# Reordering TensorE's queue in the attention stage: the scores of two steps next to each other, ahead of the values

## The chip, the core and the metric

The kernel runs on one core of one Trainium2 chip. The metric is the device time of the whole kernel in microseconds (us), from the first to the last instruction and what lies around them; the kernel has one launch. The engines are TensorE (PE), VectorE (DVE), ScalarE (ACT), GpSimd (POOL) and SyncE (SP), which runs the DMA queue that loads and stores.

## The reference, cut to what matters

Two layers follow each other. The first is a differential attention over 4 batches of 512 tokens with 8 heads, times a gate that comes from a second attention and a mixture of 8 experts. The second layer (a state-space scan and a second mixture) is not touched by the change. The part that the change concerns:

```python
# layer 0, attention, for every batch and head: 512 queries, 512 keys, head size 8 (twice)
L1 = einsum('bhnd,bhmd->bhnm', l2norm(q1), l2norm(k1)) * cos_scale
L2 = einsum('bhnd,bhmd->bhnm', l2norm(q2), l2norm(k2)) * cos_scale
G  = tanh(delta_gain * (L1 - L2))
A1 = softmax(L1 + G);  A2 = softmax(L2 - G)
y  = einsum('bhnm,bhmd->bhnd', A1 - lambda_full * A2, v)
...
# layer 0, mixture of experts, tokens of each expert
h = relu(xf @ W1[e] + b1[e]);  out = out + m * (h @ W2[e] + b2[e])
```

## The kernel before, in words

The second of the kernel's stages computes the attention and, in the same instruction stream, the experts' blocks. Every engine has a written-out order of its own, and semaphores join them. An engine takes its instructions in the order written, so one that waits holds up all behind it.

The work is cut into **steps**, **units** and **passes**. A step is 128 keys by 512 queries of one head and one batch. A unit is four steps, that is all 512 keys of one head and batch; in the code `st` counts steps and `u = st // 4` counts units. A pass is a pair of heads: 8 units, 32 steps. There are four passes, q = -1, 0, 1, 2. The first (q = -1, `first=True`) has no expert blocks beside it, but at its start VectorE also works out where each token's row goes (`route`). Passes 0 and 1 are one hardware loop, pass 2 is written out again with `final=True`. In passes 0 to 2 each unit carries one block of 128 tokens through an expert.

What is done for a step, and by whom:

- TensorE: `difference(st)` computes L1 - L2 into `bank_d[st % 2]` (line 873, one matmul of 112 rows); `scores(st)` computes L1 and L2 into the two halves of `bank_l[st % 2]` (lines 878 and 879, two matmuls of 48 rows that lie in two different halves of the array and run at the same time).
- ScalarE: `gate(st)` is the tanh, `bank_d` to `gt` (line 998).
- VectorE: `sums(st)` computes L1 + G and L2 - G (the second half is stored with its sign turned), from `bank_l` and `gt` into `tt` (lines 1055 and 1056, two instructions).
- ScalarE: `exps_of_two(st)` takes the exponential of two steps in one instruction (line 1005), `tt` to `ex`.

Since there are two banks of scores, `scores(st)` may start only when the sums of step st - 2 are done:

```python
def scores(q, st):                      # on TensorE
    pe.wait_ge(s_T, step(q, st - 1))    # s_T counts sums: those of steps 0 .. st-2 are done
```

For a unit: `weigh(u, pair)` multiplies two steps' exponentials with the values into `bank_pv` (line 927; four matmuls of 32 columns side by side, written as eight instructions; the values of a unit take pair 0 and pair 1). ScalarE's `keep(u)` copies `bank_pv` to `pvs` after pair 1 (line 1010), TensorE's `turn(u)` transposes it back into `bank_pv` (line 935), and VectorE's `settle(u)` reduces it (line 1063). The next unit's `weigh(., 0)` may start only when `settle` is done. In the iteration with number u of the TensorE loop the scores are those of steps 4u+4 to 4u+7, while `weigh` and `turn` belong to unit u-1.

For an expert block: `turn_block` (line 902), ScalarE's `keep_in` (1014), `hidden` (908), VectorE's `relu` (1071), `block_out` (914), ScalarE's `keep_out` (1019), then again `turn_block` of the next block, which uses the same bank and so waits for `keep_out`.

ScalarE's order around the change, for one unit: gates of steps 4u+4 and 4u+5, `keep(u-1)`, exponentials of 4u+2 and 4u+3, `keep_out(u)`, gates of 4u+6 and 4u+7, `keep_in(u+1)`, exponentials of 4u+4 and 4u+5. VectorE's: sums of 4u+4, sums of 4u+5, `settle(u-1)`, sums of 4u+6, sums of 4u+7, `relu(u+1)`. At steps 14 and 30 of a pass a `mean_square` (line 1129) stands between the sums of 4u+6 and of 4u+7, and at steps 5 and 21 a reciprocal (line 1125) behind `settle`.

SyncE loads the operands of the second head of a pass (`second_head`, line 716) behind two of the block loads; POOL prepares a head's values (`next_head`, line 780) when the last unit that reads the old ones has been weighed, and then the rows of the blocks, for which the block loads wait.

Of the kernel before, what the change touches and what calls it, by code (L numbers as in the profile page):

```python
# [46 lines left out]
def build_stages(nc, A, out):  # L47
    keep = ExitStack()
    with keep:
# [25 lines left out]
        with keep0:  # L75
# [561 lines left out]
            with st2:  # L637
# [60 lines left out]
                with nc.Block() as block:  # L698
# [159 lines left out]
                    def _(pe):  # L858
# [3 lines left out]
                        def operands(q, st):  # L862
                            u, mb = st // 4, st % 4
                            i, b = (u // 4) % 2, u % 4
                            if st % 16 == 0 and st > 0:
                                pe.wait_ge(s_ld[i], q * (16 * LOADS) + 32 * LOADS)
                            k = slice(512 * b + P * mb, 512 * b + P * mb + P)
                            return kst[i], qst[i], k, slice(512 * b, 512 * b + 512)

                        def difference(q, st):  # L870
                            ks, qs, k, n = operands(q, st)
                            pe.wait_ge(s_G, step(q, st - 1))
                            nc.tensor.matmul(bank_d[st % 2][:, :], ks[:, k], qs[:, n], start=True, stop=True).then_inc(s_D, 1)  # L873

                        def scores(q, st):
                            ks, qs, k, n = operands(q, st)
                            pe.wait_ge(s_T, step(q, st - 1))
                            nc.tensor.matmul(bank_l[st % 2][:, 0, :], ks[0:48, k], qs[0:48, n], start=True, stop=True)
                            nc.tensor.matmul(bank_l[st % 2][:, 1, :], ks[64:112, k], qs[64:112, n], start=True, stop=True).then_inc(s_L, 1)

                        def rank_tokens():
                            pe.wait_ge(s_ones, 1)
                            pe.wait_ge(s_cst, 16 * 4)
                            pe.wait_ge(s_cum, 1)
                            rank_bank = bank_e[:, :, :].rearrange("p t d -> p (t d)")
                            nc.tensor.matmul(rank_bank[:, 0:P], below[:, :], mask0[:, :, :].rearrange("p t e -> p (t e)"), start=True, stop=False)
                            nc.tensor.matmul(rank_bank[:, 0:P], ones[:, :], cum[0][:, 0:NT, :].rearrange("p t e -> p (t e)"), start=False, stop=True)
                            nc.tensor.matmul(rank_bank[:, P:P + NE], ones[:, :], cum[0][:, NT, :], start=True, stop=True).then_inc(s_rk, 1)

                        def turn_mask():  # L890
                            pe.wait_ge(s_rows, 2)
                            nc.tensor.transpose(bank_e[:, 0, :], mask0[:, :, :].rearrange("p t e -> p (t e)"), ident[:, :]).then_inc(s_rk, 1)

                        def bias_of_tokens(b):
                            pe.wait_ge(s_rows, 3 + b)
                            nc.tensor.matmul(bank_e[:, :, :], maskT[:, :], b2blk[:, 4 * b:4 * b + 4, :], start=True, stop=True).then_inc(s_rk, 1)

                        def turn_block(q, k):
                            pe.wait_ge(s_xl[k % 2], loaded(q, k))
                            pe.wait_ge(s_ek, blk(q, k))  # L900
                            pe.wait_ge(s_rows, 7)
                            nc.tensor.transpose(bank_e[:, 0, :], xb[k % 2][:, 0:D], ident[:, :]).then_inc(s_xt, 1)

                        def hidden(q, k):
                            pe.wait_ge(s_xk, blk(q, k + 1))
                            pe.wait_ge(s_wl[k % 2], loaded(q, k))
                            for f in range(4):
                                last = nc.tensor.matmul(bank_e[:, f, :], w1[k % 2][:, P * f:P * f + P], xbT[:, :], start=True, stop=True)
                            last.then_inc(s_h, 1)

                        def block_out(q, k):
                            pe.wait_ge(s_relu, blk(q, k + 1))
                            for f in range(4):
                                last = nc.tensor.matmul(bank_e[:, 0, :], hid[:, f, :], w2[k % 2][:, f, :], start=(f == 0), stop=(f == 3))
                            last.then_inc(s_dn, 1)

                        def weigh(q, u, pair):
                            i, b = (u // 4) % 2, u % 4
                            if pair == 0:
                                pe.wait_ge(s_yb, unit(q, u))  # L920
                                pe.wait_ge(s_vh, q * 2 + (3 + u // 4))
                            pe.wait_ge(s_E, step(q, 4 * u + 2 * pair + 2))
                            for m in range(2):
                                for s in range(2):
                                    j = 2 * s + m
                                    mb = 2 * pair + m
                                    last = nc.tensor.matmul(bank_pv[32 * j:32 * j + 32, :], vh[i][:, 4 * b + mb, :], ex[:, u % 2, mb, s, :],  # L927
                                                            start=(pair == 0), stop=(pair == 1), tile_position=(0, 32 * j), skip_group_check=True)
                            if pair == 1:
                                last.then_inc(s_pvd, 1)  # L930

                        def turn(q, u):
                            pe.wait_ge(s_pvs, unit(q, u + 1))
                            for t in range(4):
                                last = nc.tensor.transpose(bank_pv[:, P * t:P * t + P], pvs[:, P * t:P * t + P], ident[:, :])
                            last.then_inc(s_pvt, 1)

                        def pair_of_heads(q, first=False, final=False):
                            for u in range(UNITS):
                                more = not (final and u == UNITS - 1)  # L940
                                before = not (first and u == 0)
                                if not first:
                                    turn_block(q, u)
                                if before:
                                    weigh(q, u - 1, 0)
                                if more:
                                    difference(q, 4 * u + 4)
                                    difference(q, 4 * u + 5)
                                if not first:
                                    hidden(q, u)  # L950
                                elif u == 3:
                                    turn_mask()
                                elif u > 3:
                                    bias_of_tokens(u - 4)
                                if more:
                                    scores(q, 4 * u + 4)
                                if before:
                                    weigh(q, u - 1, 1)
                                if more:
                                    scores(q, 4 * u + 5)  # L960
                                if first and u == 0:
                                    rank_tokens()
                                if more:
                                    difference(q, 4 * u + 6)
                                    difference(q, 4 * u + 7)
                                if not first:
                                    block_out(q, u)
                                if more:
                                    scores(q, 4 * u + 6)
                                if before:  # L970
                                    turn(q, u - 1)
                                if more:
                                    scores(q, 4 * u + 7)

                        for st in range(4):
                            difference(-1, st)
                            scores(-1, st)
                        pe.wait_ge(s_zv, 4)
                        pair_of_heads(-1, first=True)
                        with pe.Fori(0, 2) as q:  # L980
                            pair_of_heads(q)
# [1075 lines left out]
        with st5:  # L2057
# [36 lines left out]
            more = lambda l, n: not (l == 3 and n >= 4)  # L2094
# [599 lines left out]
```

## Time and profile before

| | |
|---|---|
| time, median of 3 runs | 1299.53 us (1299.25 to 1301.14) |
| time of the profiled execution | 1300.58 us |
| its span, first to last instruction | 1298.7 us |
| busy over the whole span: PE, DVE, ACT, POOL | 88%, 84%, 80%, 73% |
| first pass of heads, from full TensorE clock | about 120 to 163 us |
| passes 0 to 2 | about 163 to 333 us |
| granted TensorE clock in both | 1.00 |

How to read it: the attention stage is some 235 us of the 1298.7, from about 103 to 338 us. What lies behind it starts when it has ended. The share of busy time of the whole kernel says little about this stage, so the rows further down are of this stage alone. A matmul's record is longer than the time it keeps the array, since its end is modelled and the next one's start lies before it; distances between starts are what counts on TensorE.

### The profile page before, as it was taken

What the parts mean: (1) busy time and instruction counts of PE and PEld (TensorE: products, weight loads), DVE (VectorE), ACT (ScalarE), POOL (GpSimd) and SP (SyncE); (2) the same over time, 40 slices, a digit from 0 to 9 for tenths busy, and PEclk for the clock granted to TensorE, in tenths of its full rate; (3) what the DMA queues carried; (4) which work ended last, traced back from release to release, by engine and by line L of the source; (5) the groups of instructions that cost most, each with busy time, mean ns of one, the idle gap of its engine ahead of it and who ended that gap; (6) DMA issues with size and microseconds to landing.
All of it is one profiled execution on the core that took longest, in us unless ns stands there. A gap on an engine that the chain in (4) does not pass through costs nothing. (4 is left out here: it accounts for less than half of the span.)

```text
span 1298.7 us, 21475 instructions
## 1 busy us (share of the span) xinstructions
PE 1148.5 (88%) x6651; PEld 610.9 (47%) x6651; DVE 1085.2 (84%) x1509; ACT 1042.7 (80%) x1803; POOL 945.7 (73%) x822
## 2 busy tenths in 40 slices
PE   6467999999669999977999999999999999999885
PEld 4462245455345556743445444444444454444442
DVE  8967989999664222359999999999999999999996
ACT  4336999999642243488999999999999999999992
POOL 6733444444442541477999999999999999999995
PEclk9786999999859999989999999999999999999998
DMA  2022234343146027334325423451444254234420
GB/s 66 28 95 94 81 89 126 115 127 98 37 159 218 21 66 178 111 89 98 91 60 108 113 64 68 106 126 53 87 110 93 59 109 112 67 64 106 108 66 16
DMA packets 87972, 119.51 MB, mean 92 GB/s; under 512 B 18171, under 2 KB 48359, under 8 KB 87488
## 3 DMA queue, kind: packets, MB, share of 16 engines
q1 hardware_dynamic: 81344, 100.90, 30.7%
q0 software_dynamic: 6528, 17.40, 4.5%
q8 instruction: 48, 0.79, 0.3%
q14 instruction: 52, 0.43, 0.1%
HBM read 92.09 MB, written 27.47 MB: 92 GB/s over the span
## 5 line engine op out<-in xcount | busy, mean ns | idle before, releaser
L2212 POOL TENSOR_TENSOR hcm<-hs,Cc 128x1024 f32<-128x1024 f32 x255 | 601.0, 2381 | 27.9 <-DVE hs L2595 19.7
L2595 DVE TENSOR_TENSOR_SCAN hs<-decay,dbx 128x512 f32<-128x512 f32 x512 | 587.1, 1200 | 26.2 <-ACT decay L2488 9.5
L2329 PEld LDWEIGHTS dbx<-ident_sb,scaled 128*128 128x128 f32 x2048 | 226.8, 142 | 288.9 <-DVE hs L2595 163.5
L2329 PE MATMUL dbx<-ident_sb,scaled 128*128 128x128 f32 x2048 | 311.7, 282 | 41.9 <-DVE hs L2595 38.6
L2470 ACT ACTIVATE scaled<-duT,BT 128x256 f32<-128x256 f32 x579 | 266.5, 505 | 0.2 <-PE dbx L2329 0.2
L2488 ACT ACTIVATE decay<-dtr_odd,a_all 128x512 f32<-128x512 f32 x256 | 178.3, 723 | 3.5 <-DMA dtr_odd<-dt_turn 2.4
L2488 ACT ACTIVATE decay<-dtr_even,a_all 128x512 f32<-128x512 f32 x256 | 177.8, 717 | 3.0 <-DVE hs L2595 1.7
L2347 PE MATMUL y_bank<-hcm,fold_sb 128*32 128x512 f32 x1024 | 138.7, 614 | 1.6 <-POOL hcm L2212 1.6
L1005 ACT ACTIVATE ex<-tt 128x2048 f32<-128x2048 f32 x64 | 123.2, 1925 | 2.5 <-DVE tt L1056 1.8
L2260 PE MATMUL slots<-XT,w_tap 128*128 128x512 f32 (+1 forms) x224 | 115.4, 597 | 3.1 <-DVE scaled L2586 2.9
L2197 POOL TENSOR_SCALAR scaled<-duT,BT 128x256 f32<-128x256 f32 x204 | 96.3, 487 | 0.0
L1055 DVE TENSOR_TENSOR tt<-bank_l,gt 128x512 f32<-128x512 f32 x128 | 87.0, 680 | 6.2 <-ACT gt L998 4.5
L998 ACT ACTIVATE gt<-bank_d,dgh 128x512 f32<-128x512 f32 x128 | 82.3, 708 | 7.7 <-PE bank_d L873 7.7
L1056 DVE SCALAR_TENSOR_TENSOR tt<-bank_l,gt 128x512 f32<-128x512 f32 x128 | 86.9, 679 | 0.0
L1957 DVE TENSOR_TENSOR hid<-sil,u_bank 128x512 f32<-128x512 f32 x32 | 22.0, 687 | 59.4 <-ACT sil L1814 37.7
L927 PE MATMUL bank_pv<-ex,v_head 128*32 128x512 f32 x512 | 68.8, 611 | 2.3 <-DVE ybig L1063 1.5
L2586 DVE TENSOR_TENSOR scaled<-slots,BT 128x1024 f32<-128x1024 f32 (+1 forms) x60 | 67.8, 1130 | 0.0
L1814 ACT ACTIVATE sil<-g_bank 128x512 f32<-128x512 f32 x32 | 19.1, 597 | 47.3 <-PE u_bank L1671 47.2
L2047 DVE TENSOR_TENSOR hid<-sil,u_bank 128x320 f32<-128x320 f32 x32 | 15.6, 487 | 48.8 <-ACT sil L1900 48.8
L1635 POOL DMA_INDIRECT shares_of_tokens<-eo,to_u x18 | 17.2, 956 | 51.8 <-ACT eo L1937 48.2
L1627 POOL DMA_INDIRECT expert_rows<-XR,rows_u x32 | 31.3, 978 | 31.1 <-PE o_bank L1678 21.8
L2347 PEld LDWEIGHTS y_bank<-hcm,fold_sb 128*32 128x32 f32 x1024 | 20.3, 108 | 48.4 <-issue 40.3
(386 smaller groups left out, 1886.3 us busy)
## 6 DMA issues: line engine op xcount, KB each, us to landing
Cc<-bc_turn SPq DMA_DIRECT2D x256, 64.0 KB, 2.2
dtr_even<-dt_turn SPq DMA_DIRECT2D x32, 512.0 KB, 8.6
dtr_odd<-dt_turn SPq DMA_DIRECT2D x32, 512.0 KB, 8.9
dt_turn<-dt SPq DMA_DIRECT2D x16, 512.0 KB, 2.8
hid<-in_conv_row SPq DMA_DIRECT2D x4, 512.0 KB, 5.3
shares_of_tokens<-zeros SPq DMA_DIRECT2D x2, 1024.0 KB, 8.0
w_rg<-in_w_rg SPq DMA_DIRECT2D x8, 256.0 KB, 2.9
w_ru<-in_w_ru SPq DMA_DIRECT2D x8, 256.0 KB, 3.1
```

The lines of the kernel that those rows point to most:

```text
L998: nc.scalar.activation(gt[:, st % RING, :], bank_d[st % 2][:, :], ACT.Tanh, scale=dgh[:, i:i + 1]).then_inc(s_G, 1)
L1005: nc.scalar.activation(ex[:, (st // 4) % 2, j:j + 2, :, :], tt[:, i:i + 2, :, :], ACT.Exp).then_inc(s_E, 2)
L1055: nc.vector.tensor_tensor(tt[:, st % RING, 0, :], bank_l[st % 2][:, 0, :], gt[:, st % RING, :], ALU.add)
L1056: nc.vector.scalar_tensor_tensor(tt[:, st % RING, 1, :], bank_l[st % 2][:, 1, :], -1.0, gt[:, st % RING, :], ALU.mult, ALU.subtract).then_ ...
L2197: nc.gpsimd.tensor_scalar(scaled[buffer_of(l, n, k)][:, kk, :, j, :], duT[:, n % 2, kk, :].rearrange("p (g c) -> p g c", c=32), BT[:, n % ...
L2212: nc.gpsimd.tensor_tensor(hcm[:, r - 1:r + 1, :], hs[:, p % HR - 1:p % HR + 1, :], Cc[:, k:k + 1, :].broadcast_to([P, 2, 512]), ALU.mult). ...
L2260: last = mm(dst[h][:, d:512], w_tap[:, 3 - d, P * h:P * h + P], XT[:, n % 4, 0:512 - d], start=(d == 0), stop=(d == 3))
L2329: last = nc.tensor.transpose(dbx[bank_of[p]][:, P * kk:P * kk + P], scaled[buffer_of(l, b, k)][:, kk, g, :, :].rearrange("p j c -> p (j c) ...
L2347: last = mm(y_bank[h][32 * q:32 * q + 32, :], fold[:, :], hcm[:, ring_of(l, b, p + q), :], start=False, stop=(k == 3), tile_position=(0, 3 ...
L2470: nc.scalar.activation(scaled[buffer_of(l, n, k)][:, kk, :, j, :], duT[:, n % 2, kk, :].rearrange("p (g c) -> p g c", c=32), ACT.Copy, sca ...
L2488: nc.scalar.activation(dec[:, p % DR, :], dtr[b % 2][:, g, :], ACT.Exp, scale=a_all[:, l, 4 * g + k:4 * g + k + 1]).then_inc(s_dec, 1)
L2595: nc.vector.tensor_tensor_scan(hs[:, p % HR, :], dec[:, p % DR, :], dbx[bank_of[p]][:, :], 0.0, ALU.mult, ALU.add).then_inc(s_sc, 1)
```

## The change

Only TensorE's order within a unit changes; no instruction is added, removed or resized, and no wait is edited. `scores` of step 4u+5 moves from behind `weigh(u-1, 1)` to ahead of it, directly behind `scores` of step 4u+4. `scores` of step 4u+6 moves from ahead of `turn(u-1)` to behind it, so that it stands directly ahead of `scores` of step 4u+7, and `turn(u-1)` stands directly behind `block_out(u)`.

```diff
                                 if more:
                                     scores(q, 4 * u + 4)
+                                    scores(q, 4 * u + 5)
                                 if before:
                                     weigh(q, u - 1, 1)
-                                if more:
-                                    scores(q, 4 * u + 5)
                                 if first and u == 0:
                                     rank_tokens()
                                 if more:
                                     difference(q, 4 * u + 6)
                                     difference(q, 4 * u + 7)
                                 if not first:
                                     block_out(q, u)
-                                if more:
-                                    scores(q, 4 * u + 6)
                                 if before:
                                     turn(q, u - 1)
                                 if more:
+                                    scores(q, 4 * u + 6)
                                     scores(q, 4 * u + 7)
```

In the first iteration of the first pass there is no `weigh` and no `turn`, and its order stays as it was.

## Rows read from the trace of the kernel before

**Rows 1.** Windows of the first pass, and of one unit in passes 0, 2, -1.

```profile
core 0: us, PE busy (x) PEld busy (x) DVE busy (x) ACT busy (x) POOL busy (x), PEclk, DMA share, GB/s
120.00:163.00 43.00, 38.37 (x224) 11.31 (x223) 39.50 (x72) 42.55 (x48) 21.49 (x26) 1.00 0.24 74
...
207.80:214.91 7.11, 7.05 (x49) 3.58 (x49) 6.42 (x13) 6.82 (x10) 5.24 (x10) 1.00 0.39 113
285.30:292.31 7.01, 7.01 (x52) 3.58 (x50) 6.51 (x15) 6.84 (x10) 2.65 (x5) 1.00 0.49 152
144.45:150.85 6.40, 5.96 (x39) 1.78 (x35) 5.82 (x11) 6.40 (x9) 3.85 (x7) 1.00 0.58 176
```

**Rows 2.** Timeline of PE, one unit of pass 0 (start us, us long).

```profile
207.80 1.07 PE L927 MATMUL bank_pv<-ex,v_head 128*32 128x512 f32 x8
...
210.23 0.39 PE L878 MATMUL bank_l<-GATE 48*128 48x512 bf16 x1
...
210.55 1.06 PE L927 MATMUL bank_pv<-ex,v_head 128*32 128x512 f32 x8
...
211.87 0.61 PE L873 MATMUL bank_d<-GATE 112*128 112x512 bf16 x2
212.31 1.06 PE L914 MATMUL bank_e<-expert_weights,hid 128*128 128x128 f32 x8
...
213.62 0.66 PE L935 MATMUL bank_pv<-ident_sb,pvs 128*128 128x128 f32 x4
...
214.53 0.33 PE L902 MATMUL bank_e<-ident_sb,block_in 128*128 128x128 f32 x1
214.91 1.06 PE L927 MATMUL bank_pv<-ex,v_head 128*32 128x512 f32 x8
```

**Rows 3.** Timeline of ACT in the same unit.

```profile
211.68 0.60 ACT L1010 ACTIVATE pvs<-bank_pv 128x512 f32<-128x512 f32 x1 [0.29 <-PE bank_pv L927]
...
213.97 0.27 ACT L1019 ACTIVATE block_out<-bank_e 128x128 f32<-128x128 f32 x1
214.13 1.27 ACT L998 ACTIVATE gt<-bank_d,dgh 128x512 f32<-128x512 f32 x2
```

**Rows 4.** Timeline of DVE: sums of two steps, settle, and mean_square.

```profile
207.78 0.69 DVE L1055 TENSOR_TENSOR tt<-bank_l,gt 128x512 f32<-128x512 f32 x1
...
209.58 0.68 DVE L1056 SCALAR_TENSOR_TENSOR tt<-bank_l,gt 128x512 f32<-128x512 f32 x1
...
214.42 0.44 DVE L1063 TENSOR_REDUCE ybig<-bank_pv 128x272 f32 x1 [0.48 <-PE bank_pv L935]
214.91 0.69 DVE L1055 TENSOR_TENSOR tt<-bank_l,gt 128x512 f32<-128x512 f32 x1
...
216.12 0.41 DVE L1129 TENSOR_REDUCE ms<-ysq 128x256 f32 x1
216.44 0.68 DVE L1055 TENSOR_TENSOR tt<-bank_l,gt 128x512 f32<-128x512 f32 x1
```

**Rows 5.** Timeline of ACT: copies of weighed values, and a gate, in all passes.

```profile
121.71 0.60 ACT L1010 ACTIVATE pvs<-bank_pv 128x512 f32<-128x512 f32 x1 [0.45 <-PE bank_pv L927]
...
153.70 0.61 ACT L1010 ACTIVATE pvs<-bank_pv 128x512 f32<-128x512 f32 x1
...
155.99 1.27 ACT L998 ACTIVATE gt<-bank_d,dgh 128x512 f32<-128x512 f32 x2
...
167.29 0.60 ACT L1010 ACTIVATE pvs<-bank_pv 128x512 f32<-128x512 f32 x1 [0.51 <-PE bank_pv L927]
...
190.12 0.60 ACT L1010 ACTIVATE pvs<-bank_pv 128x512 f32<-128x512 f32 x1 [1.19 <-PE bank_pv L927]
...
325.41 0.60 ACT L1010 ACTIVATE pvs<-bank_pv 128x512 f32<-128x512 f32 x1 [0.16 <-PE bank_pv L927]
```

**Rows 6.** Timeline of DVE, the sums of step 7 in the first pass.

```profile
120.20 0.68 DVE L1056 SCALAR_TENSOR_TENSOR tt<-bank_l,gt 128x512 f32<-128x512 f32 x1
```

**Rows 7.** Timeline of SP's queue: the block load ahead of a head's load.

```profile
168.20 0.32 SPq L710 DMA_DIRECT2D block_in<-block_rows  x1
```

**Rows 8.** Timeline of PE: the first matmul that uses the loaded head.

```profile
187.24 0.60 PE L873 MATMUL bank_d<-GATE 112*128 112x512 bf16 x2 [1.21 <-DMA GATE<-qk_parts]
```

## The prediction

> **What bounds the kernel now.** I read the page first (which engines are busy, and when), then windows of the attention stage, then the timelines of PE, ACT and DVE over one unit, because with three engines near full the order of the queues decides and not the busy shares. In the windows [rows 1] the reader should compare each engine's busy time with the unit's length. A unit of passes 0 and 1 takes 7.11 us, PE is busy 7.05 of it and ACT 6.82. In pass 2 it is 7.01, with PE at 7.01. In the first pass, which has no expert blocks, a unit takes 6.40 us, and there ACT is busy all 6.40 and PE only 5.96. So two limits lie close together: PE bounds the passes with expert blocks, ACT the pass without, and ACT has 0.29 us of slack per unit, all of it in front of the copy of the weighed values [rows 3].
>
> PE's own 7.11 us hold one more wait: `weigh(., 0)` starts at 214.91, 0.05 us after `settle` ends at 214.42 + 0.44 = 214.86 [rows 2, 4].
>
> **What the change does, part by part.**
>
> *Nothing is added.* The matmuls, their sizes and all waits stay. The two moves change what stands behind what.
>
> *`scores(4u+6)` behind `turn`.* `turn` starts one pair of scores earlier, 0.32 us (the distance from `scores` to what follows it, 210.23 to 210.55 [rows 2]). `settle` then ends 0.32 us earlier against `weigh(., 0)`, which frees the wait of PE just named. `turn` needs the copy `pvs`; the copy starts at 211.68 and lasts 0.60 [rows 3], while `turn` starts at 213.62 [rows 2], so it can come earlier. The sums of step 4u+6 start when the gate has come (214.13 to 214.91 [rows 3, 4]) and don't notice that their scores come later, since ACT is later too, as follows.
>
> *`scores(4u+5)` ahead of `weigh(., 1)`: the dear part.* These scores wait for the sums of step 4u+3. Before, this wait cost nothing, as it stood behind `weigh`, and what followed it was not urgent. Now the wait stands in front of `weigh`, and behind `weigh` hangs all of ACT's queue: the copy, the exponentials, `keep_out`, the next gates. From those gates come the sums of 4u+6 and 4u+7, and for the latter the next unit's `scores(4u+9)` wait. That closes a ring, from one `weigh(., 1)` to the next:
>
> - start of `weigh` to start of the copy: 210.55 to 211.68, 1.13 [rows 2, 3]
> - copy to gates, with exponentials and `keep_out` between: 211.68 to 214.13, 2.45 [rows 3]; in the first pass, without `keep_out`, 153.70 to 155.99, 2.29 [rows 5]
> - gate to the sums that use it: 214.13 to 214.91, 0.78 [rows 3, 4]
> - the sums of two steps, start to end: 207.78 to 209.58 + 0.68 = 210.26, 2.48 [rows 4]
> - DVE's end to PE's start: 0.05, as behind `settle`
> - `scores(4u+9)` to `weigh`: 0.32 [rows 2]
>
> Sum: 7.21 us in passes 0 to 2, and 7.05 in the first. In the old order the ring closed over `scores(4u+8)`, which needs one step's sums less and has no second pair of scores behind it, and so had about a microsecond to spare. In the new one it is longer than the present unit: by 0.10 in passes 0 and 1 (7.11), by 0.20 in pass 2 (7.01), by 0.65 in the first pass (6.40). `mean_square` stands between the two sums, twice a pass, and adds 216.12 to 216.44 = 0.32 [rows 4] each time; before it was hidden.
>
> Now the terms, by the copy's start, once per unit:
>
> 1. Entering, in the first pass. The sums of step 7 end at 120.20 + 0.68 = 120.88 [rows 6]. Scores of step 9 start at 120.93, `weigh` at 121.25, the copy at 122.38, where it was at 121.71 [rows 5]: +0.67.
> 2. From that copy to the one at 167.29 [rows 5] are seven units: 45.58 us before, 7 x 7.05 + 0.32 (step 30) = 49.67 after: +4.09.
> 3. To the copy at 190.12. One unit in here waits 1.21 us for the second head's operands, needed at 187.24 [rows 8]. Their load begins behind the block load at 168.20 [rows 7], for which POOL's preparation of the head must be through, and that waits for the `weigh` in front of 167.29. So the load moves with that copy (+4.76), and the wait hides the ring's excess and one `mean_square`. Behind the loaded operands one more pair of scores now comes ahead of `weigh`: +0.32.
> 4. From 190.12 to 325.41 [rows 5] are 19 units, 135.29 us before, and 19 x 7.21 + 4 x 0.32 = 138.27 after: +2.98.
> 5. The last units have no scores to come, and I leave them at what they take.
>
> Sum: 0.67 + 4.09 + 0.32 + 2.98 = +8.1 us. What follows the stage starts when it ends, so nothing takes it back. The span goes from 1298.7 to about 1306.8, the profiled execution from 1300.58 to 1308.7; this execution lies 1.05 above the median of the runs, and against the median 1299.53 the forecast is **1307.6 us**.
>
> **Prices that the trace doesn't show.** Two pairs of scores back to back without a wait occur nowhere at full clock. Two differences take 0.44 together, 0.22 each (211.87 to 212.31), and a pair of scores, whose two matmuls run side by side and are of the same 512 columns, 0.32 [rows 2]. Their distance is then 0.22 at the least (it can't stream faster than one matmul) and 0.39 at most (a pair's whole record). I take 0.22 to 0.32, and it doesn't enter the sum: PE stands waiting for the sums in front of the second pair whichever it is. Only the distance from scores to `weigh` enters, and that is measured. At 0.39 on both the ring would be 0.07 longer, 26 x 0.07 = 1.8 us in all.
> `keep_out` to `turn_block` is a second way around: 213.97 + 0.27 + 0.05 = 214.29 less 210.55 gives 3.74 from `weigh`, then `turn_block` to the next `weigh(., 0)` 0.38 (it holds part of the old wait), 207.80 to 210.23 is 2.43, two pairs of scores 0.64 at most: 7.19, just under the ring. So that is no bound of its own, and a shortened ring would find it only 0.02 below, or 0.2 lower with the cheaper prices.
>
> The row's difference of 0.32 and 0.22 agrees with a rule, and this one speaks for the change: the Trainium skill, TensorEngine Tiling (Array Packing), Key Properties, says that switching the array's tiling mode drains it. Scores use half-height tiles, the values narrow ones, the rest the full array, and the change takes three of ten switches out of a unit. By rule and rows PE would need some 0.3 us less per unit, and that is the first rival below; I hold that PE no longer sets the unit.
>
> **Rivals.**
>
> *PE's switches and the freed wait decide: faster.* Three switches at 0.32 - 0.22 = 0.10 each give a PE unit of 6.8 us. ACT's 6.82 to 6.84 would bound [rows 1]. Gain 0.28 x 16 + 0.17 x 8 = 5.9 us, the first pass unchanged as ACT is full there: 1293.6 us. For it: PE is at 7.05 of 7.11 busy. Against it: the ring must be at most 6.84, 0.37 shorter than its rows, and in the first pass 0.65 shorter. It decides from where the sums of 4u+3 end ahead of the first pair's start.
>
> *The two cancel: the same.* Were each turn of the ring 0.25 us shorter (by overlaps I don't see), passes 0 and 1 would run at 6.96, a gain of 16 x 0.15 = 2.4, and the first pass at 6.80, a loss of 7 x 0.4 = 2.8. 1299.5 to 1300.5 us.
>
> *TensorE's clock falls in the first pass: slower still.* PE would be busy 5.96 of 7.05 us there, 85% (now 93%). The windows show 1.00 from 120 on [rows 1], with the 1.21 us wait inside it. One unit at the lower of the two levels would need 11.9 us of PE, +4.9: 1312.5 or more.
>
> *The change does nothing:* no, for the waits meet in every unit.
>
> **Chances and range.** My forecast 0.80, with a range of its own of 1305.7 to 1309.5 (0.07 us on each of 26 turns). Faster by PE 0.08, the two cancel 0.06, clock 0.06. 0.2%, which is 2.6 us, is about what a measurement of this kernel can tell from no change. Slower takes the forecast and the clock, 0.86; same 0.06; faster 0.08. The range, 1304.0 to 1311.0, takes in the unknown prices and a partly hidden `mean_square`, and leaves out under 2 in 10.
>
> **What would show it.** In the profile after, PE should sit in front of the second pair of scores, released by DVE's sums, in every unit. The copy's distance from one unit to the next should be 7.05 in the first pass and 7.21 later, 0.32 more at steps 14 and 30. ACT's gap before the copy should be 0.65 in the first pass (none now) and 0.4 later. The wait for `settle` should be gone. The wait for the head's operands should remain, but shorter. I am wrong if the second pair starts directly behind the first, if the first pass keeps its 6.40, or if the sums start sooner behind the gates than 0.78.

## The result and the profile after

The changed kernel takes 1308.57 us (median of 6, 1307.14 to 1310.12) where the kernel before takes 1300.97 (median of 6, 1299.25 to 1302.78, the three runs shown ahead of the prediction among them). The ratio is 1.0062 with a 95% interval of 1.0052 to 1.0073: slower by some 8 us, with 1307.6 forecast. The profiled execution took 1310.12 us with a span of 1308.3, the longest of the six.

Line numbers of the changed kernel are lower by 2 from this place on: the gate is L996, the copy of the weighed values L1008, the sums L1053 and L1054.

The timelines of one ordinary unit of pass 0 after the change, first PE, then ACT, then DVE, answer to [rows 2], [rows 3] and [rows 4]:

```profile
208.59 0.39 PE L878 MATMUL bank_l<-GATE 48*128 48x512 bf16 x1
...
209.04 0.39 PE L878 MATMUL bank_l<-GATE 48*128 48x512 bf16 x1
...
209.36 1.07 PE L927 MATMUL bank_pv<-ex,v_head 128*32 128x512 f32 x8
...
210.80 1.06 PE L914 MATMUL bank_e<-expert_weights,hid 128*128 128x128 f32 x8
211.69 0.60 PE L935 MATMUL bank_pv<-ident_sb,pvs 128*128 128x128 f32 x4
212.22 0.39 PE L878 MATMUL bank_l<-GATE 48*128 48x512 bf16 x1
...
212.46 0.39 PE L878 MATMUL bank_l<-GATE 48*128 48x512 bf16 x1
...
213.15 0.30 PE L902 MATMUL bank_e<-ident_sb,block_in 128*128 128x128 f32 x1 [0.30 <-ACT block_out L1017]
213.38 1.07 PE L927 MATMUL bank_pv<-ex,v_head 128*32 128x512 f32 x8
...
216.26 0.39 PE L878 MATMUL bank_l<-GATE 48*128 48x512 bf16 x1
...
216.58 1.07 PE L927 MATMUL bank_pv<-ex,v_head 128*32 128x512 f32 x8
```
```profile
210.49 0.60 ACT L1008 ACTIVATE pvs<-bank_pv 128x512 f32<-128x512 f32 x1 [0.38 <-PE bank_pv L927]
...
212.94 1.27 ACT L996 ACTIVATE gt<-bank_d,dgh 128x512 f32<-128x512 f32 x2
```
```profile
213.72 0.69 DVE L1053 TENSOR_TENSOR tt<-bank_l,gt 128x512 f32<-128x512 f32 x1 [0.82 <-ACT gt L996]
...
215.52 0.68 DVE L1054 SCALAR_TENSOR_TENSOR tt<-bank_l,gt 128x512 f32<-128x512 f32 x1
```

Follow the ring: `weigh` at 209.36, copy at 210.49 (1.13), gate at 212.94 (2.45), sums at 213.72 (0.78), their end at 215.52 + 0.68 = 216.20 (2.48), the second pair of scores at 216.26 (0.06), the next `weigh` at 216.58 (0.32). That is 7.22 us. The second pair starts 0.45 us behind the first at 208.59, though behind `turn` a pair follows a pair in 212.46 - 212.22 = 0.24: PE stands in front of it for the sums. The profile shows no idle there, since 0.39 of the 0.45 is covered by the record of the pair before. Only where the wait is longer, as at `mean_square`, is it printed. PE has one more wait here, 0.30 us in front of `turn_block` for `keep_out`. It costs nothing, since the second pair behind it waits for the sums in any case.

Windows of the first pass, of two ordinary units of passes 0 and 2, and of one of the first pass:

```profile
120.00:168.00 48.00, 40.46 (x233) 11.23 (x231) 39.36 (x72) 43.25 (x49) 21.30 (x26) 1.00 0.22 67
209.36:216.58 7.22, 6.86 (x51) 3.56 (x50) 6.35 (x14) 6.84 (x10) 3.15 (x7) 1.00 0.46 139
297.11:304.33 7.22, 6.86 (x51) 3.56 (x50) 6.27 (x14) 6.84 (x10) 3.15 (x7) 1.00 0.46 142
148.95:156.00 7.05, 6.17 (x36) 1.72 (x34) 5.81 (x11) 6.50 (x9) 0.00 (x0) 1.00 0.01 5
```

Against [rows 1]: now no engine fills a unit. PE has 6.86 of 7.22 and ACT 6.84. In the first pass ACT, full before, has 6.50 of 7.05. The clock stays at 1.00 there.

### The profile page after: what moved, and what is told of

It reads as the page before. It is cut to its first block and busy times, and to the rows that moved or that the text cites. A ratio compares the mean times of both kernels' runs of the same rounds, so it can differ in the third digit from the quotient of the medians.

```text
span 1308.3 us, 21475 instructions
## 1 busy us (share of the span) xinstructions
PE 1151.7 (88%) x6651; PEld 615.0 (47%) x6651; DVE 1084.9 (83%) x1509; ACT 1043.2 (80%) x1803; POOL 944.6 (72%) x822
## 5 line engine op out<-in xcount | busy, mean ns | idle before, releaser
L1053 DVE TENSOR_TENSOR tt<-bank_l,gt 128x512 f32<-128x512 f32 x128 | 87.5, 684 | 27.1 <-ACT gt L996 25.7
L996 ACT ACTIVATE gt<-bank_d,dgh 128x512 f32<-128x512 f32 x128 | 81.8, 701 | 7.6 <-PE bank_d L873 7.5
L1054 DVE SCALAR_TENSOR_TENSOR tt<-bank_l,gt 128x512 f32<-128x512 f32 x128 | 87.0, 680 | 0.0
```

What stands on the lines that cost most here:

```text
L996: nc.scalar.activation(gt[:, st % RING, :], bank_d[st % 2][:, :], ACT.Tanh, scale=dgh[:, i:i + 1]).then_inc(s_G, 1)
L1053: nc.vector.tensor_tensor(tt[:, st % RING, 0, :], bank_l[st % 2][:, 0, :], gt[:, st % RING, :], ALU.add)
L1054: nc.vector.scalar_tensor_tensor(tt[:, st % RING, 1, :], bank_l[st % 2][:, 1, :], -1.0, gt[:, st % RING, :], ALU.mult, ALU.subtract).then_ ...
```

## The experiments

The kernel before was run beside each group of experiments. Its median is 1300.42 us (24 runs) for the first four kernels and 1299.90 (9 runs) for the next four; the second profile of the changed kernel has one run of the kernel before beside it. Ratios are to these, so between groups they are the numbers to compare, and not the medians. Edits are shown cut to what matters, against the changed kernel where nothing else is said.

**One part alone: the pair ahead of the values** (against the kernel before).

```diff
                                     scores(q, 4 * u + 4)
+                                    scores(q, 4 * u + 5)
                                 if before:
                                     weigh(q, u - 1, 1)
-                                if more:
-                                    scores(q, 4 * u + 5)
```

> One part of the change alone: the scores of step 4u+5 go ahead of the values, while turn stays behind the scores of 4u+6. The ring theory (the values wait for the second pair of scores, which waits for the sums of 4u+3, which hang on the gates behind the last unit's copy): the unit is as long as with both parts, 7.05 to 7.06 us in the first pass and 7.22 later, 7.55 at steps 14 and 30, so the time is that of the whole change, 7 to 8.5 us above the kernel before, ratio 1.005 to 1.007. Rival (the late scores of 4u+6, or the earlier turn, are what costs): units as before, 6.40 and 7.11, ratio within 0.999 to 1.002.

Measured: 1308.66 us, ratio 1.0066 (1.0053 to 1.0079). Copies of successive units in its trace (L1009 in this kernel):

```profile
142.55 0.60 ACT L1009 ACTIVATE pvs<-bank_pv 128x512 f32<-128x512 f32 x1 [0.55 <-PE bank_pv L927]
...
149.60 0.60 ACT L1009 ACTIVATE pvs<-bank_pv 128x512 f32<-128x512 f32 x1 [0.55 <-PE bank_pv L927]
...
202.12 0.60 ACT L1009 ACTIVATE pvs<-bank_pv 128x512 f32<-128x512 f32 x1 [0.38 <-PE bank_pv L927]
...
209.35 0.60 ACT L1009 ACTIVATE pvs<-bank_pv 128x512 f32<-128x512 f32 x1 [0.38 <-PE bank_pv L927]
```

Distances of 7.05 and 7.23, as with the whole change. This part alone brings the whole loss.

**The other part alone: turn early, the later pair behind it** (against the kernel before).

```diff
                                     block_out(q, u)
-                                if more:
-                                    scores(q, 4 * u + 6)
                                 if before:
                                     turn(q, u - 1)
                                 if more:
+                                    scores(q, 4 * u + 6)
                                     scores(q, 4 * u + 7)
```

> The other part alone: turn goes directly behind block_out and the scores of 4u+6 and 4u+7 follow each other behind it, while the scores of 4u+5 stay behind the values. Ring theory: the ring closes over one step's sums less, about 6.0 us, and binds nowhere. PE sheds two switches between half-height tiles and the full array and the wait for settle, so that ScalarE's 6.82 to 6.84 us of work are the unit in passes 0 to 2; the first pass keeps 6.40. 16 x 0.28 + 8 x 0.17 = 5.9 us less than before: ratio 0.9945 to 0.997. Rival (this part costs): slower than before by 2 us or more. Rival (PE bounds all the same): 7.0 to 7.1 per unit, ratio 0.998 to 1.000.

Measured: 1296.03 us, ratio 0.9971 (0.9960 to 0.9983), so faster, by 4.4 us where 5.9 were expected. ACT in its trace (its copy is L1009):

```profile
202.35 0.60 ACT L1009 ACTIVATE pvs<-bank_pv 128x512 f32<-128x512 f32 x1
...
209.13 0.60 ACT L1009 ACTIVATE pvs<-bank_pv 128x512 f32<-128x512 f32 x1
...
216.01 0.60 ACT L1009 ACTIVATE pvs<-bank_pv 128x512 f32<-128x512 f32 x1
...
223.53 0.60 ACT L1009 ACTIVATE pvs<-bank_pv 128x512 f32<-128x512 f32 x1 [0.57 <-PE bank_pv L927]
```

No gap stands in front of most copies; their distances alternate 6.78 and 6.88 here, and are 6.82 to 6.84 elsewhere. ACT bounds. Some units still wait: 223.53 - 216.01 = 7.52 at the hardware loop's jump, where the kernel before takes 7.35, and three more of 7.11 to 7.21. Together they hold about the missing 1.5 us.

**Both pairs next to each other, but the first behind the values.**

```diff
-                                if more:
-                                    scores(q, 4 * u + 4)
-                                    scores(q, 4 * u + 5)
                                 if before:
                                     weigh(q, u - 1, 1)
+                                if more:
+                                    scores(q, 4 * u + 4)
+                                    scores(q, 4 * u + 5)
```

> Both pairs of scores next to each other as in the change, turn early, but the first pair stands behind the values instead of ahead of them: weigh(u-1, 1), scores 4u+4, scores 4u+5, differences. If the place ahead of the values is what costs (ring theory), the loss is gone and the unit falls to ScalarE's 6.82 to 6.85 us, 6.40 in the first pass: 5 to 6 us below the kernel before, ratio 0.9945 to 0.997. If it is the scores' being next to each other that costs (two banks of scores, the second pair waiting for sums), the units stay at 7.05 and 7.22 and the ratio at 1.005 to 1.007.

Measured: 1297.68 us, ratio 0.9986 (0.9977 to 0.9995). The loss is gone, as expected, but the gain is about half of the least that I expected: a unit of passes 0 to 2 takes 6.98 us, and two units of the first pass take 6.71 instead of 6.40. PE and then DVE in its trace:

```profile
206.06 0.39 PE L878 MATMUL bank_l<-GATE 48*128 48x512 bf16 x1 [0.18 <-DVE tt L1054]
...
210.06 0.39 PE L878 MATMUL bank_l<-GATE 48*128 48x512 bf16 x1
...
210.29 0.38 PE L878 MATMUL bank_l<-GATE 48*128 48x512 bf16 x1
...
213.03 0.39 PE L878 MATMUL bank_l<-GATE 48*128 48x512 bf16 x1 [0.18 <-DVE tt L1054]
```
```profile
210.49 0.69 DVE L1053 TENSOR_TENSOR tt<-bank_l,gt 128x512 f32<-128x512 f32 x1
...
212.30 0.68 DVE L1054 SCALAR_TENSOR_TENSOR tt<-bank_l,gt 128x512 f32<-128x512 f32 x1
```

Here another ring closes over two steps' sums. The first pair at 210.06 gives the sums at 210.49, these end at 212.98, and the last pair of the unit (4u+7), which needs them, starts at 213.03: 2.97 us. Behind it come `turn_block`, `weigh(., 0)`, two differences, `hidden` and `weigh(., 1)` before the next first pair, 4.00 us more (from 206.06, where the last pair of the unit before starts, to 210.06). Sum 6.97. So with two banks of scores a pair next to another can cost behind the values too, when both steps' sums lie in a ring with PE. This ring is read from one trace; no run cuts it.

**The changed order kept, the ring cut on ACT.** The buffer of the sums has 8 slots instead of 4 (`WIDE`), the lead of the counters is 8, and four gates stand ahead of the loop.

```diff
                             for st in range(0, STEPS, 2):
...
-                                if not (final and st == STEPS - 2):
+                                ahead = mb == 2 and not (final and st == STEPS - 2)
+                                if ahead:
                                     gate(q, st + 2)
                                     gate(q, st + 3)
...
                                     keep(q, u - 1)
-                                exps_of_two(q, st)
+                                if ahead:
+                                    gate(q, st + 4)
+                                    gate(q, st + 5)
                                 if mb == 2 and not first:
                                     keep_out(q, u)
+                                exps_of_two(q, st)
```

> TensorE's order of the change is kept as it is, and the ring is cut on ScalarE: behind the copy come the gates of 4u+6 and 4u+7 and keep_out, and only then the exponentials (1.80 us); the buffer for the sums has 8 slots instead of 4, so that the sums needn't wait for those exponentials. Ring theory: the ring is 1.80 + 0.16 shorter, about 5.3 us, and the unit falls from 7.22 to ScalarE's 6.82 to 6.85, from 7.06 to about 6.4 in the first pass; 4 to 6 us below the kernel before, ratio 0.995 to 0.998. Rival (the scores' order costs on TensorE itself): units stay near 7.2, ratio above 1.004.

Measured: 1296.15 us, ratio 0.9972 (0.9963 to 0.9982). PE in its trace, in the changed order:

```profile
208.71 0.39 PE L878 MATMUL bank_l<-GATE 48*128 48x512 bf16 x1
...
208.94 0.38 PE L878 MATMUL bank_l<-GATE 48*128 48x512 bf16 x1
...
209.25 1.06 PE L927 MATMUL bank_pv<-ex,v_head 128*32 128x512 f32 x8
```

The second pair now follows the first in 0.23, so nothing is waited for, and the copies of later units lie 6.76 and 6.80 apart. TensorE's order of the change isn't slow in itself; it is slow with the old order on ACT. The edit changes two things, the order and the buffer, and the buffer was not run alone. In the changed kernel, though, the sums wait for the gate (the row at 213.72 above) and not for a slot, so the longer buffer by itself had nothing to free there. At the start of the first pass this version loses some: the first copy waits 2.21 us for PE, and the units there lie between 6.38 and 6.84 apart.

**The first pass in the old order.** The whole change, with `scores(4u+5)` behind `weigh` when `first`.

```diff
                                     scores(q, 4 * u + 4)
+                                if more and not first:
                                     scores(q, 4 * u + 5)
                                 if before:
                                     weigh(q, u - 1, 1)
+                                if more and first:
+                                    scores(q, 4 * u + 5)
```

> The whole change, except that in the first pass (no expert blocks) the scores of 4u+5 stay behind the values. It splits the sum into its terms. Ring theory: the first pass goes back to 6.40 us a unit, which takes off the 0.67 us of entering and the 4.1 to 4.2 us of its seven units; passes 0 to 2 keep 7.22 and 7.55. Remaining loss against the kernel before: 0.3 (behind the head's load) + 3.0 to 3.4 = 3 to 4 us, ratio 1.002 to 1.0035. Rival (the loss of the first pass comes from turn's place, or from the clock): the ratio stays at 1.005 or more.

Measured: 1305.00 us, ratio 1.0039 (1.0024 to 1.0053). Its copies from the one at 121.52 to the one at 159.91 lie 6.36 to 6.43 apart. The copies of the seven units from 121.52 on take 45.73 us in all, against 49.81 with the whole change: 4.1 us back, as expected. By the ratios it is 1.0062 - 1.0039, 3.0 us, and the remaining loss lies above the 1.002 to 1.0035 expected; the intervals are too wide to tell 3 from 4.8. In the trace the stage's last copy comes 3.1 us later than before, inside the 3 to 4 expected; the span is 4.5 longer, and the rest of it lies behind the stage.

**mean_square out of the ring.**

```diff
-                                if st == 14 and not first:
+                                if st == 15 and not first:
                                     mean_square(q * 2 + 1, q * 12 + 11)
...
-                                if st == 30:
+                                if st == 31:
                                     mean_square(q * 2 + 2, q * 12 + 17)
```

> The whole change, with mean_square moved on VectorE from between the sums of steps 14 and 15 (30 and 31) to behind those of 15 (31), so out of the ring. Ring theory: no unit of 7.55 us and none of 7.38 is left in the stage, all are 7.22 (first pass 7.06); where the head's load decides nothing changes. 5 x 0.33 = 1.6 us below the whole change, ratio to the kernel before 1.004 to 1.0055. Rival (VectorE's spare time hides mean_square, and the long units have another cause, the head's end or the block's load): the 7.55 us units stay.

Measured: 1308.03 us, ratio 1.0061 (1.0048 to 1.0075). The trace shows what was expected: `mean_square` behind both sums, and no unit of 7.55 left.

```profile
215.20 0.60 ACT L1008 ACTIVATE pvs<-bank_pv 128x512 f32<-128x512 f32 x1 [0.39 <-PE bank_pv L927]
...
222.42 0.60 ACT L1008 ACTIVATE pvs<-bank_pv 128x512 f32<-128x512 f32 x1 [0.39 <-PE bank_pv L927]
```

This is the unit at step 30 of pass 0, 7.22 instead of 7.55. The stretch from the unit behind the head's load to the last but two (19 units, 193.53 to 330.94) takes 137.41 us where the changed kernel takes 138.63, so 1.2 us less, for four units. The times don't show it: the ratio is 1.0061 after 1.0062, above the 1.004 to 1.0055 expected, though the interval reaches down to 1.0048. The term is shown by the trace and not by the times.

**The changed kernel again, twice.**

> The changed kernel itself once more, for a second profile. In the first one TensorE's granted clock fell behind the wait for the second head's operands in pass 0, and that unit took 9.93 us where the ring and the load alone give about 8.7. If the fall is tied to this wait it comes again, and the unit is again 9.5 us or more; if it is chance, the unit is 8.7 to 9.3 us and the span about 1 us shorter than 1308.3.

This execution took 2327.22 us, with TensorE's matmuls some twice as long in all stages and 97% busy, while ScalarE's copies took their usual 0.60 us. Beside it the kernel before took 1299.90 on the same chip, and the six runs of the changed kernel in the result took 1307 to 1310. What caused it is open. It isn't used.

> The changed kernel itself, since the look before this one came out at 2327 us with every matmul some twice as long, beside runs of the kernel before at 1299.9 us on the same chip, and says nothing on the question. The same question: in the first profile the unit with the head's load took 9.93 us, of which 1.28 us of waiting and some 1.2 us of a lower TensorE clock behind it. If that is tied to the wait, it comes again (9.5 us or more); if it is chance, 8.0 to 9.3 us. All other units must again be 7.05 to 7.06, 7.22, and 7.55 at steps 14 and 30.

Measured: 1311.11 us, beside one run of the kernel before at 1302.87. From the second unit on all are as expected, but for the ones at a pass's end (7.16) and at the hardware loop's jump (7.32), which the first profile has too. The one with the head's load takes 7.96 us, just under the 8.0 to 9.3 expected, and the clock is 1.00 in it. First the changed kernel's first profile, then this one:

```profile
188.00:196.00 8.00, 6.47 (x36) 2.93 (x35) 5.26 (x13) 5.07 (x8) 2.50 (x4) 0.79 0.30 94
```
```profile
188.00:196.00 8.00, 6.84 (x52) 3.51 (x50) 6.79 (x15) 6.87 (x10) 2.73 (x6) 1.00 0.31 94
```

So the fall of the clock in the first profile isn't tied to that wait. But the clock fell elsewhere in the second, early in the first pass. There PE had waited 0.41 and 0.81 us for the sums and been busy 0.84 of the 2.00 us from 126 to 128 (in the first profile 0.93 of 2.00, and the clock held):

```profile
126.00:128.00 2.00, 0.84 (x8) 0.32 (x12) 1.53 (x4) 2.00 (x3) 1.41 (x2) 1.00 0.10 33
129.00:131.00 2.00, 2.00 (x12) 0.90 (x10) 1.45 (x3) 1.75 (x2) 1.40 (x2) 0.50 0.19 64
```

The unit there, the first, took 7.30 us instead of 7.05. The version with `mean_square` behind has the same fall at the same place, with 7.48. The profiles of the six other experiments show none between 126 us and the stage's end, nor does the kernel before. Whether the changed order makes such falls likelier is open; they cost about 1.6 us in the first profile (see the terms below) and 0.25 in the second.

**A version from these results.** In the first pass the old order on ACT and `scores(4u+5)` behind the values; ACT's gates go ahead of the exponentials from the first pass's last unit on, and TensorE has the changed order from pass 0 on.

```diff
+                                old = first and st < STEPS - 2
-                                ahead = mb == 2 and not (final and st == STEPS - 2)
-                                if ahead:
+                                ahead = mb == 2 and not (final and st == STEPS - 2) and not old
+                                if ahead or old:
                                     gate(q, st + 2)
                                     gate(q, st + 3)
```

(against the version with the gates ahead; TensorE's part as in "The first pass in the old order", and two of the four gates ahead of the loop are gone again)

> What the experiments so far point to, as a version: in the first pass TensorE keeps the scores of 4u+5 behind the values and ScalarE its old order; from the last unit of the first pass on TensorE has the changed order and ScalarE the gates and keep_out ahead of the exponentials, with 8 slots for the sums. Both parts then run at ScalarE's own work: 6.40 us a unit, then 6.78 (only_turn_early: 6.83). About 1 us below only_turn_early: 1294.5 to 1296, ratio 0.995 to 0.997. If ScalarE is not the bound in the later passes, no gain over it, or a loss.

Measured: 1294.87 us, ratio 0.9966 (0.9952 to 0.9979). It is the lowest median of all. By the ratios it lies 0.0005, some 0.65 us, below the early turn alone, and the two intervals overlap almost wholly, so no gain over it is shown. Both beat the kernel before; the early turn alone does it with two moved lines.

## Why the prediction was right

**The ring.** Predicted 7.21 us, measured 7.22; in the first pass 7.05 and 7.05 to 7.06; with `mean_square` 0.33 more where 0.32 was predicted. All six hops measure as in the rows of before, the last but one 0.06 for 0.05. Cutting the ring at either end (the pair behind the values, the gates ahead of the exponentials) takes the loss away, and the pair ahead of the values alone brings all of it. The cause is shown.

**The terms**, from the first weighing of the kernel before and then of the changed kernel, and from the copies in the changed kernel's first profile:

```profile
117.48 1.93 PE L927 MATMUL bank_pv<-ex,v_head 128*32 128x512 f32 x8
```
```profile
116.95 1.94 PE L927 MATMUL bank_pv<-ex,v_head 128*32 128x512 f32 x8
```
```profile
121.86 0.60 ACT L1008 ACTIVATE pvs<-bank_pv 128x512 f32<-128x512 f32 x1 [1.12 <-PE bank_pv L927]
...
171.67 0.60 ACT L1008 ACTIVATE pvs<-bank_pv 128x512 f32<-128x512 f32 x1 [0.48 <-PE bank_pv L927]
...
196.05 0.60 ACT L1008 ACTIVATE pvs<-bank_pv 128x512 f32<-128x512 f32 x1 [2.86 <-PE bank_pv L927]
...
334.68 0.60 ACT L1008 ACTIVATE pvs<-bank_pv 128x512 f32<-128x512 f32 x1 [0.38 <-PE bank_pv L927]
```

1. Entering: 121.86 against 121.71 [rows 5], in an execution in which the stage began 0.53 earlier (the first `weigh` at 116.95, before at 117.48): +0.68, predicted 0.67. The pair ahead alone gives +0.68 too. This holds where the clock reaches 1.00 by about 120 us, as in these three. In the second profile it did so at about 121.4, and entering took 1.73 more than before.
2. First pass: 49.81 us for seven units, predicted 49.67, against 45.58 before: +4.23.
3. To the unit with the head's load: 24.38 against 22.83 before, +1.55, predicted 0.32. This term missed, in size. The clock fell here, and without that, in the second profile, the stretch took 22.40, 0.43 less than before. My step "the load moves with that copy" holds for the load's start: the block load ahead of it starts 0.91 us behind the copy before, and 0.90, 0.90 and 0.89 in the two profiles of the changed kernel and the one with the pair ahead alone. It doesn't hold for its end: from the copy to the operands' arrival it is 19.95 us before, and 19.68, 19.31 and 20.60 in these three. A load that ends 1.3 us sooner or later is part of what the times scatter by. From the arrival to the next copy it is 2.88 us before and 3.09 and 3.10 where the clock held, so the one more pair costs some 0.22 and not 0.32: unstalled, a pair follows a pair in 0.23. With the fallen clock it was 4.70.
4. The 19 units behind it: 138.63, predicted 138.27, against 135.29: +3.34. The missing 0.36 is 19 times 0.01, four times 0.01 at `mean_square` and 0.11 at the hardware loop's jump.

Sum 9.8 us, where the profiled spans differ by 9.6; by medians it is 7.6, with 8.1 predicted. The profiled execution had the fall of the clock on top.

How near the total comes is partly luck. The same sum is 9.1 us in the second profile (1.73 + 4.48 - 0.43 + 3.35) and with the pair ahead alone (0.68 + 4.24 + 0.87 + 3.34), so the stage lost 1.0 to 1.7 us more than I added up, by the head's load, the clock and the entry. It also began 0.5 to 1.5 us earlier in these three than in the one profile of the kernel before, which takes most of it off again, though the change doesn't touch what lies ahead. Behind the stage the spans scatter as well: with the pair ahead alone the last copy comes 8.1 us later and the span is 6.0 longer. The ring's two terms, 2 and 4, are the solid part: 7.07 us forecast, 7.57, 7.58 and 7.83 measured.

Two slips of mine on the side, which the forecast doesn't use: 0.28 x 16 + 0.17 x 8 is 5.8 and not 5.9, and `turn` starts 0.42 earlier behind `block_out` (1.31 before, 0.89 now) and not 0.32, since a switch of tiling goes with the pair. The second way around, over `keep_out`, measures 3.79 + 0.23 + 2.43 + 0.55 = 7.00 where I had 7.19; it is no bound here.

**PE's side.** The unstalled distance between two pairs was bounded at 0.22 to 0.39 and taken as 0.22 to 0.32; it is 0.23 to 0.24. It didn't enter the ring. A `turn` behind `block_out` starts 211.69 - 210.80 = 0.89 behind it, where half-height scores before started 0.99 behind it. I read the difference, about 0.10, as the price of a switch of tiling; no run isolates it from what else differs between the two instructions. That agrees with the rule of the Trainium skill (TensorEngine Tiling (Array Packing), Key Properties) on draining. The change saved three switches per unit, and PE stood waiting instead.

**The rivals.** Faster by PE's switches: refuted for the change. Half of the change is faster, as the early turn alone shows (0.9971), though how much of that is switches and how much the freed wait wasn't told apart. The clock in the first pass: refuted as the cause, for it is 1.00 from 120 to 168 us in the first profile and the units take 7.05 all the same; but it did fall once there in the second profile, for 0.25 us of time and not 4.9. The two cancel: refuted by the ring's length and by the ratio's interval.

**What the profile should have shown.** The wait for `settle` is gone: `weigh(., 0)` starts 0.23 behind `turn_block`, with the settle long done. ACT's gap in front of the copy is 0.38 in passes 0 to 2 (0.4 predicted), but 0.55 in the first pass for 0.65: ACT is busy 6.50 there and not 6.40, since the end of the gate's record is no longer covered by the copy. The wait for the head's operands was to be shorter. It was 1.28 in the first profile, 0.91 in the second and 2.18 with the pair ahead alone, for 1.21 before, so that isn't shown: the load's end scatters by more.

## What to carry to other kernels

When several engines are near full, add up the ring of waits from an instruction back to itself in the next iteration, and compare it with the iteration's length: a move that puts a wait in front of an instruction on which another engine's whole queue hangs lengthens the ring even if it shortens the engine's own work. Two instructions of a kind next to each other with only two buffers between them and their reader put two readers' times into the ring. The same move costs nothing any more once the ring is cut elsewhere, here by gates ahead of the exponentials. Whether it then brings anything isn't shown, as the gates ahead were not run without it. Test the parts of an edit alone: here one half lost 8 us and the other won 4.

## What the runs showed of the hardware

A wait of PE can be hidden in the profile: two pairs that follow each other in 0.23 us when free lie 0.45 apart, with no idle time printed. TensorE's granted clock fell once behind a 1.28 us wait for a DMA (0.79 over 188 to 196 us, `hidden` 1.92 us long instead of 1.06). In nine other profiles, with waits of 0.91 to 2.18 us at the same place, it didn't. In two of them it fell to 0.50 at about 128 us instead, behind waits of 0.41 and 0.81 us for VectorE. One execution had all matmuls about twice as long while its records gave the clock as 1.00, and I can't explain it.
